# Second attention: the banks of the early projections, and the place of the matmuls that sum the probabilities

## The chip, the cores and the metric

The kernel runs on one core of a Trainium2 chip. Its time is the device time of one execution in microseconds (us); before the change the median of three runs is 2448.55 us (2448.41 to 2448.85). Five engines work side by side: PE (TensorE, matmuls; its weight loads stand in the profile as PEld), DVE (VectorE), ACT (ScalarE), POOL (GpSimd) and SP (SyncE, which issues the DMAs). Each engine runs its own list of instructions in order, and semaphores join them. Matmuls write to PSUM, which is eight banks of 128 x 512 fp32; DVE and ACT read the results from there.

## What is computed

The reference is four layers, each an attention and a feed-forward part, on x of 4 x 256 x 256 with a context of 4 x 1601 x 256. The change touches only the attention of the layer numbered 2, "the second attention":

```python
q = rms_norm((x @ wq).reshape(B, L, 16, 128), q_norm_w)
k, v = x @ wk, x @ wv                      # 4 heads of 128
k_ctx, v_ctx = ctx @ wk_ctx, ctx @ wv_ctx  # 4 heads of 128; k and k_ctx through rms_norm
q, k = q * cos + rotate_half(q) * sin, k * cos + rotate_half(k) * sin
scores = einsum(q, concat([k_ctx, k])) / sqrt(128) + causal
out = einsum(softmax(scores), concat([v_ctx, v]))
return out.reshape(B, L, 2048) @ wo
```

Each key head serves four query heads. There are 1601 + 256 keys, which make 15 chunks of up to 128.

## The kernel before

The second attention runs in 16 **turns**, one for each batch and key head (`TURNS = B * KH`), with a turn ahead of them that only prepares. Turn g does the attention of head g and beside it prepares head n = g + 1. A turn has 29 **steps** (`NS`), one for each pair of a tile of 128 queries (k = 0, 1) and a chunk of keys it sees: 14 steps for k = 0 (c = 0 to 13) and 15 for k = 1 (c = 14 to 28). The order of the work is written out by hand, by step, for each engine.

At step c of turn g, PE issues in this order:
- `project` (L1654 to L1671): at steps 2 to 16, the projection of one chunk of keys and values of the **next** head, two matmuls of 256 columns in fp32, which run as four passes (L1670). At steps 23 and 25 a projection of queries (L1651) instead.
- `search` (L1757 to L1766): one or two pieces of the maximum search of the next head, from step 11 on; the first before or after the scores, the second behind the values (L1764, L1765).
- `scores` of step c + 3 (L1699 to L1701), into banks 0 to 2 in turn.
- `values` of step c (L1704 to L1718): three matmuls of 512 columns, V high with P high (L1715), V low with P high (L1716), V high with P low (L1718), which add into bank 3 for k = 0 and bank 4 for k = 1.
- `sums` (L1720 to L1728): the probabilities of a query tile, added up on POOL in `l2_acc` (L1322), are summed over the keys by four matmuls of one column, fp32, so eight weight loads and eight passes (L1727). Those of k = 0 stand at step 21 of the same turn, those of k = 1 at step 1 of the next (`SUM_AT = [21, 1]`), behind the values of that step; at step 21 behind the second search piece too.
- `output` (L1747), `maxima` (L1754, at step 6 for k = 1 and step 24 for k = 0) and the transposes of the preparation (L1777, L1790).

A projection or search piece takes its PSUM bank from a list, `BANKS` (L1213), which goes by the item's place in the order `SHARED`. Before the change the first 23 items (the projections of steps 2 to 16 and the eight search pieces among them) go to banks 5 and 6 in turn, the rest to 3, 5, 6. `bank_free` (L1631) makes PE wait, ahead of the item's first weight load, until the last earlier item of the same bank has been read. For a projection that is the DVE subtraction that makes V low (L1533), which follows two ACT copies (L1422, L1423); for a search piece the DVE maximum (L1540). The first item on a bank in a turn waits for the last one of the turn before; the first on bank 3 waits on `l2_o` for the ACT copy of the finished k = 0 output.

That copy is `products` (L1401 to L1404): ACT reads bank 3 or 4 into `l2_oT` and adds one to `l2_o`. That of k = 0 runs at step 15 of its turn, that of k = 1, which reads bank 4, at step 1 of the **next** turn (`PV_AT`), where it stands behind `exp` of step 3 (L1364, L1365) and the seed of a score bank (L1376) in ACT's order.

Of the kernel before, what the change touches and what calls it, by code (L numbers as in the profile page):

```python
# [17 lines left out]
P = 128  # L18
B, S, D = 4, 256, 256
DC = D // P  # L20
TB = S // P
# [63 lines left out]
def program(nc, t, out):  # L85

    with ExitStack() as stack:

        def sem(name):
            return stack.enter_context(nc.semaphore(name))  # L90
# [4 lines left out]
        def sb(name, shape, dt=F32, scope=stack):  # L95
            return scope.enter_context(nc.sbuf_tensor(name, shape, dt))
# [3 lines left out]
        def bank(n, width=BANK, at=0):  # L100
            return psum[:, n * BANK + at:n * BANK + at + width]
# [12 lines left out]
        ones = sb("ones", [P, P])  # L114
# [25 lines left out]
        x_upd = sem("x_upd")  # L140
# [3 lines left out]
        xT_cp = sem("xT_cp")  # L144
# [10 lines left out]
        X_AT = [sum(UPDATES[:k]) for k in range(len(UPDATES) + 1)]  # L155
# [948 lines left out]
        KG = -(-KC // 4)  # L1104
# [3 lines left out]
        TURNS = B * KH  # L1108
# [14 lines left out]
        l2_acc, l2_oT = parts[:TB], parts[TB:]  # L1123
# [38 lines left out]
        NS = len(STEPS)  # L1162
        TILE_END = [max(c for c in range(NS) if STEPS[c][0] == k) for k in range(TB)]
# [22 lines left out]
        SUM_AT = [21, 1]  # L1186
        Y_AT = [(26, 28), (3, 5)]
        LAST_SUM, LAST_Y = 5, [(7, 6), (7, (NS - 3) % 3)]

        def max_pieces(c):  # L1190

            return [(k, h, q) for k, q, first, n in SEARCH_AT.get(c, []) for h in range(first, first + n)]
# [13 lines left out]
        def shared_at(c):  # L1206

            return ([("project", c)] if TB <= c < NPROJ else []) + [("query", k) for k in range(TB) if QUERY_AT[k] == c] \
                + [("search", SEARCH.index(piece)) for piece in max_pieces(c)]

        SHARED = [item for c in range(NS) for item in shared_at(c)]
        PAIR = sum(len(shared_at(c)) for c in range(NPROJ))
        BANKS = [5 + at % 2 for at in range(PAIR)] + [(3, 5, 6)[(at - PAIR) % 3] for at in range(PAIR, len(SHARED))]  # L1213
        EARLY_PROJECTS = 3
        FIRST_SHARED = [("project", k) for k in range(TB)] + SHARED
        LAST_ON_FIVE = TB + sum(len(shared_at(c)) for c in range(LATE_FROM))
# [3 lines left out]
        def is_first(n):  # L1220

            return isinstance(n, int) and n == 0

        def sequence(n):

            return (FIRST_SHARED, FIRST_BANKS) if is_first(n) else (SHARED, BANKS)

# [12 lines left out]
        def last_in(n, b, before=None):  # L1240

            items, of = sequence(n)
            return max((at for at in range(before or len(items)) if of[at] == b and (following(n) is not None or items[at][0] != "query")),
                       default=-1)
# [386 lines left out]
        def bank_free(pe, kind, i, n):  # L1631
            items, of = sequence(n)
            own = items.index((kind, i))
            at = last_in(n, of[own], own) if own else -1
            if at >= 0:
                wait_freed(pe, items[at], n)
            elif is_first(n):
                if own >= LAST_ON_FIVE:
                    pe.wait_ge(h_cp, HALF_CP[1])
            elif of[own] == 3:  # L1640
                pe.wait_ge(l2_o, (n - 1) * TB + 1)
            else:
                wait_freed(pe, sequence(n - 1)[0][last_in(n - 1, of[own])], n - 1)

# [28 lines left out]
        def l2x_tensor(pe):  # L1673
# [27 lines left out]
                pe.matmul(dst, l2_kTlo[slot][:, keys], l2_qThi[slot][:, k, :], start=False, stop=True, skip_group_check=True)\  # L1701
                    .then_inc(l2_s, 1)

            def values(g, slot, c):  # L1704
                k, j = STEPS[c]
                r = key_cols(j)[1]
                pe.wait_ge(l2_e, g * (3 * NS) + (3 * c + 1))
                if j == 0:
                    need(pe, l2_o, g * TB + (k - 1))
                if j == 0 and last_in(g, 3 + k) >= 0:  # L1710
                    wait_freed(pe, sequence(g)[0][last_in(g, 3 + k)], g)
                if k == 0:
                    pe.wait_ge(l2_vl, g * KC + (CHUNK_AT[j] + 1))
                vhi, vlo, phi = l2_vhi[slot][0:r, j, :], l2_vlo[slot][0:r, j, :], l2_phi[c % 3][0:r, :]
                pe.matmul(bank(3 + k), vhi, phi, start=(j == 0), stop=False)  # L1715
                pe.matmul(bank(3 + k), vlo, phi, start=False, stop=False)  # L1716
                pe.wait_ge(l2_lo, g * NS + (c + 1))
                pe.matmul(bank(3 + k), vhi, l2_plo[c % 3][0:r, :], start=False, stop=(j == MC + k)).then_inc(l2_pv, 1)  # L1718

            def sums(g, k, at=7):  # L1720
                pe.wait_ge(l2_accd, g * NS + (TILE_END[k] + 1))
                if at == LAST_SUM:
                    pe.wait_ge(xT_cp, TOP_CP + DONE // TB)
                elif k == 1:
                    pe.wait_ge(x_upd, g * (2 * TB) + (X_AT[4] + 2))
                for h in range(REP):
                    mm = pe.matmul(bank(at, 1, h), l2_acc[k][:, h * P:(h + 1) * P], ones[:, 0:1], start=True, stop=True)  # L1727
                mm.then_inc(l2_sum, 1)  # L1728

            def output(g, k, half):  # L1730
# [62 lines left out]
            def turn(g, slot, n):  # L1793
                for c in range(NS):
                    pieces = max_pieces(c) if n is not None else []
                    if n is not None and c >= (EARLY_PROJECTS if g is None else TB):
                        project(pe, c, n)
                    if c in QUERY_AT and following(n) is not None:
                        k = QUERY_AT.index(c)
                        if k == 0:  # L1800
                            weights_here(pe, n + 1)
                        bank_free(pe, "query", k, n)
                        project_query(pe, k, bank(shared_bank(n, "query", k)))
                    keys_turned = c - 1 in KT_AT.values()
                    if pieces and not keys_turned:
                        search(1 - slot, n, *pieces[0])
                    at, step = ahead(c, 3, g, n)
                    if at is not None:
                        scores(at, slot if c + 3 < NS else 1 - slot, step)
                    if pieces and keys_turned:  # L1810
                        search(1 - slot, n, *pieces[0])
                    if g is not None:
                        values(g, slot, c)
                    for piece in pieces[1:]:
                        search(1 - slot, n, *piece)
                    if g is not None:
                        later = not isinstance(g, int) or g >= 1
                        if c == SUM_AT[1] and later:
                            sums(g - 1, 1)
                        for half in range(2):  # L1820
                            if c == Y_AT[1][half] and later:
                                output(g - 1, 1, half)
                        if c == M1_AT:
                            if later:
                                pe.wait_ge(x_upd, g * (2 * TB) + X_AT[4])
                            maxima(g, 1)
                        if c == SUM_AT[0]:
                            if n is not None:
                                pe.wait_ge(l2_kTl, (n + 1) * KG)
                            sums(g, 0)  # L1830
                    if c == M_AT and n is not None:
                        if g is not None:
                            pe.wait_ge(l2_inv, g * TB + 1)
                        else:
                            pe.wait_ge(l2_kTl, (n + 1) * KG)
                        maxima(n, 0)
                    if g is not None:
                        for half in range(2):
                            if c == Y_AT[0][half]:
                                if n is not None and half == 0:  # L1840
                                    pe.wait_ge(l2_md, n * NSHIFT + 1)
                                output(g, 0, half)
                    if n is not None:
                        prepare(c, 1 - slot, n)
                    if last_turn(g) and c in XT_AT:
                        top_turn(pe, XT_AT[c])
                    if g is None and c == SECOND_HALF_AT[3]:
                        pe.wait_ge(h_xn, len(BLOCKS) + 2)
                        for d in range(DC):
                            attention_turn(pe, 1, d, 3 + d)  # L1850

            l2_turns_written_out(turn)
            sums(TURNS - 1, 1, LAST_SUM)
            for half in range(2):
                output(TURNS - 1, 1, half)

# [41 lines left out]
        DONE = NT - TB  # L1898
# [3 lines left out]
        TOP_K, TOP_PS, TOP_CP = norm_count["k"], norm_count["ps"], norm_count["cp"]  # L1902
# [1356 lines left out]
```

## Time and profile before

| | |
|---|---|
| median of three runs | 2448.55 us |
| the profiled execution, its own time | 2449.79 us |
| its span in the profile | 2448.0 us |
| the second attention | about 520 to 1745 us of the span |
| one full turn | 75.0 us |

Times in the rows are microseconds from the start of the span. A row of the timeline gives the start, the duration, the engine, the line and the operation with its output, inputs and shape; xN stands for N such instructions in a row, whose duration is then that from the start of the first to the end of the last. In square brackets is the idle time ahead of it and what ended it. The end of a matmul is modelled and overlaps the next one, so that for PE it is the distance from start to start that counts. A weight load is drawn from the moment it begins.

### The profile page before, as it was taken

The numbers are of one execution on the slowest core, as the hardware profiler recorded it, in microseconds if no ns is written. First come the engines' busy times: TensorE is split into PE (matmuls) and PEld (weight loads), VectorE is DVE, ScalarE is ACT, GpSimd is POOL, SyncE is SP. The second block draws the span as 40 slices with busy tenths as digits, with TensorE's granted clock in tenths as the row PEclk, the third lists the DMA queues.
The fourth block names the chain that finished last, engine by engine and source line by source line (L and its number), as shares of the span: only waits on it lengthen the run. The fifth ranks groups of instructions, "written<-read, shape, count | busy, mean of one in ns | idle before, by whom it ended". The sixth has DMA issues, their size and how long they took to land.

```text
span 2448.0 us, 50586 instructions
## 1 busy us (share of the span) xinstructions
PE 2331.0 (95%) x19062; PEld 1628.8 (67%) x19123; DVE 1740.0 (71%) x3346; ACT 1739.6 (71%) x3784; POOL 1327.3 (54%) x942
## 2 busy tenths in 40 slices
PE   7989999989999999999999999999799799999997
PEld 4677777767777777777777777777655444444444
DVE  5455767668988888888889888889411666666546
ACT  2235444458888888888888888888411688888897
POOL 1035555435666766666766667666500487878500
PEclk9989999999999999999999999999899999999999
DMA  5222322230001000010000100003200200000100
GB/s 189 70 85 84 91 86 81 78 138 13 6 18 49 18 18 1 18 49 18 18 3 17 49 18 18 18 1 138 89 28 11 72 25 16 23 17 22 55 3 18
DMA packets 42321, 108.36 MB, mean 44 GB/s; under 512 B 5060, under 2 KB 25928, under 8 KB 36936
## 3 DMA queue, kind: packets, MB, share of 16 engines
q1 hardware_dynamic: 40312, 102.28, 12.4%
q8 instruction: 156, 2.56, 0.5%
q0 software_dynamic: 768, 2.10, 0.3%
q10 hardware_dynamic: 1008, 0.79, 0.1%
q14 instruction: 77, 0.63, 0.1%
HBM read 99.78 MB, written 4.98 MB: 43 GB/s over the span
## 4 chain that ended last, share of the span: by engine, by line
PE 70%; DVE 11%; ACT 11%; issue 4%; POOL 2%; DMA 0%; another core or an unknown queue 0%; SPq 0%; ACTq 0%; DVEq 0%; POOLq 0%
PE psum L1670 6%; PE psum L2820 4%; PE psum L1765 4%; PE psum L1699 3%; PE psum L1715 3%; PE psum L1716 3%; PE psum L1718 3%; PE psum L2787 3%; PE psum L1700 3%; PE psum L1701 3%; PE psum L2184 3%; ACT l_p L2623 3%; PE psum L2753 3%; PE psum L513 2%; PE psum L515 2%
## 5 line engine op out<-in xcount | busy, mean ns | idle before, releaser
L1322 POOL TENSOR_TENSOR xn<-xn,l_p 128x512 f32<-128x512 f32 (+1 forms) x400 | 562.1, 1405 | 320.1 <-DVE l_plo L1490 308.0
L1490 DVE TENSOR_TENSOR l_plo<-l_p,l_phi 128x512 fp32r<-128x512 f32 (+1 forms) x464 | 440.4, 949 | 10.6 <-ACT l_p L1365 9.5
L2623 ACT ACTIVATE l_p<-psum 128x1024 f32<-128x1024 f32 x416 | 397.6, 1038 | 55.9 <-PE psum L2787 51.2
L1364 ACT ACTIVATE l_phi<-psum 128x512 fp32r<-128x512 f32 (+1 forms) x464 | 276.1, 595 | 100.8 <-PE psum L1701 60.1
L1540 DVE TENSOR_REDUCE l_mx<-psum 128x1 f32<-128x512 f32 (+2 forms) x512 | 303.7, 615 | 53.4 <-PE psum L1765 53.0
L1376 ACT ACTIVATE psum<-l_m 128x512 f32<-128x512 f32 x461 | 283.0, 616 | 7.9
L2598 POOL TENSOR_TENSOR l_rs<-l_ms,half_power 128x32 f32<-128x32 f32 x45 | 244.3, 5430 | 68.8 <-DVE l_ms L2648 58.7
L1365 ACT ACTIVATE l_p<-psum 128x512 f32<-128x512 f32 (+1 forms) x464 | 276.5, 596 | 0.0
L2820 PE MATMUL psum<-l_p,l_vs 64*32 64x256 f32 x6656 | 252.0, 378 | 6.9 <-POOL l_vs L2594 3.0
L1699 PE MATMUL psum<-l_qThi,l_kThi 128*128 128x512 f32 (+1 forms) x464 | 224.0, 483 | 0.9 <-ACT psum L1376 0.9
L1765 PE MATMUL psum<-l_kThi,l_qThi 128*128 128x512 f32 (+2 forms) x512 | 215.8, 450 | 6.8 <-ACT l_kThi L1457 2.3
L1670 PE MATMUL psum<-l_w,l_ctx 128*128 128x256 f32 (+1 forms) x832 | 217.6, 384 | 0.8 <-DVE l_vlo L1533 0.8
L597 POOL TENSOR_TENSOR w_lo_gu<-w_stage,w_hi_gu 128x512 fp32r<-128x512 f32 x76 | 99.7, 1312 | 163.3 <-ACT w_hi_gu L639 163.3
L1718 PE MATMUL psum<-l_plo,l_vhi 128*128 128x512 f32 (+1 forms) x464 | 184.5, 398 | 2.9 <-DVE l_plo L1490 2.9
L1715 PE MATMUL psum<-l_phi,l_vhi 128*128 128x512 f32 (+1 forms) x464 | 183.5, 395 | 0.0
L1716 PE MATMUL psum<-l_phi,l_vlo 128*128 128x512 f32 (+1 forms) x464 | 182.9, 394 | 0.0
L1700 PE MATMUL psum<-l_qTlo,l_kThi 128*128 128x512 f32 (+1 forms) x464 | 182.8, 394 | 0.0
L1701 PE MATMUL psum<-l_qThi,l_kTlo 128*128 128x512 f32 (+1 forms) x464 | 182.8, 394 | 0.0
L2787 PE MATMUL psum<-l_qT,l_kT 64*32 64x512 f16 x3328 | 171.9, 385 | 9.9 <-DVE l_qT L2447 1.5
L1670 PEld LDWEIGHTS psum<-l_w,l_ctx 128*128 128x128 f32 (+1 forms) x832 | 146.2, 187 | 25.6 <-DVE l_vlo L1533 5.9
L2820 PEld LDWEIGHTS psum<-l_p,l_vs 64*32 64x32 f32 x6656 | 118.6, 106 | 49.2 <-issue 8.5
L1765 PEld LDWEIGHTS psum<-l_kThi,l_qThi 128*128 128x128 f32 x512 | 97.7, 191 | 54.1 <-issue 23.2
(410 smaller groups left out, 5068.2 us busy)
## 6 DMA issues: line engine op xcount, KB each, us to landing
w_stage<-in_L_w_dram SPq DMA_DIRECT2D x76, 384.0 KB, 3.1
l_w<-in_L_w_qkv_dram SPq DMA_DIRECT2D x16, 1024.0 KB, 5.0
l_ct<-in_ctx_tiles_dram SPq DMA_DIRECT2D x52, 128.0 KB, 2.3
c_T<-in_ctx_T_dram SPq DMA_DIRECT2D x4, 1601.0 KB, 7.9
l_ctx<-in_ctx_T_dram SPq DMA_DIRECT2D x4, 1601.0 KB, 6.9
c_N<-in_ctx_dram SPq DMA_DIRECT2D x4, 1536.0 KB
s_wg<-in_L_gate_dram SPq DMA_DIRECT2D x4, 1024.0 KB, 10.8
s_wu<-in_L_up_dram SPq DMA_DIRECT2D x4, 1024.0 KB, 12.8
```

The source lines that it names most:

```text
L1322: g_.tensor_tensor(l2_acc[k][0:r, :], first[0:r, :], p_of(c)[0:r, :], ALU.add)\
L1364: act.activation(l2_phi[c % 3][0:r, :], src, ACT.Exp).then_inc(l2_e, 1)
L1365: act.activation(p_of(c)[0:r, :], src, ACT.Exp)\
L1376: return act.activation(bank(c % 3), l2_shift[:, STEPS[c][0], :].bitcast(F32), ACT.Copy)
L1490: v.tensor_tensor(l2_plo[c % 3][0:r, :], p_of(c)[0:r, :], l2_phi[c % 3][0:r, :].bitcast(F32), ALU.subtract)\
L1540: v.tensor_reduce(l2_mx4[:, u, q:q + 1], bank(shared_bank(n, "search", i), z - a), AX.X, ALU.max)\
L1670: mm = pe.matmul(into, lhs, l2_w[:, d, cols], start=(d == 0), stop=(d == DC - 1))
L1699: pe.matmul(dst, l2_kThi[slot][:, keys], l2_qThi[slot][:, k, :], start=False, stop=False, skip_group_check=True)
L1718: pe.matmul(bank(3 + k), vhi, l2_plo[c % 3][0:r, :], start=False, stop=(j == MC + k)).then_inc(l2_pv, 1)
L1765: pe.matmul(bank(at, z - a), l2_qThi[slot][:, k, h * P:(h + 1) * P], l2_kThi[slot][:, a:z], start=not masked, stop=True).then_inc(l2_near, 1)
L2623: act.activation(l3_p[ring(odd, c)][:, :], psum[:, (c % 2) * 2 * BANK:(c % 2 + 1) * 2 * BANK], ACT.Exp, scale=float(D3) ** -0.5).then_inc( ...
L2820: mm = pe.matmul(bank(at[a], S, cols)[h * 32:(h + 1) * 32, :], l3_vs[n % 2][rows, j, h, :], l3_p[s % 4][rows, h * S:(h + 1) * S], start=(j ...
```

## The change

Three things change.
- **Banks.** The first 11 items (the projections of steps 2 to 11 and the search piece of step 11) go to banks 4, 5 and 6 in turn. Items 11 to 22 go to 5 and 6 in turn, beginning with 5. The rest is as before. For the first projection on bank 4, that of step 2, `bank_free` waits on `l2_o` for the copy of the last turn's k = 1 output.
- **Sums.** `sums` is gone from its place; `values` takes its four matmuls in. Head 0 stands behind the first value matmul, head 1 behind the second, heads 2 and 3 behind the third. At step 21 they come ahead of the second search piece.
- **Waits.** The waits that stood ahead of `sums` (on `l2_accd`, on `x_upd` for k = 1, on `l2_kTl` for k = 0) now stand before or behind the first value matmul.

```diff
-        BANKS = [5 + at % 2 for at in range(PAIR)] + [(3, 5, 6)[(at - PAIR) % 3] for at in range(PAIR, len(SHARED))]
+        THREE_TILL = sum(len(shared_at(c)) for c in range(TILE_END[0] - 1))
+        BANKS = [4 + at % 3 for at in range(THREE_TILL)] + [5 + (at - THREE_TILL) % 2 for at in range(THREE_TILL, PAIR)] + [(3, 5, 6)[(at - PAIR) % 3] for at in range(PAIR, len(SHARED))]
...
             elif of[own] == 3:
                 pe.wait_ge(l2_o, (n - 1) * TB + 1)
+            elif of[own] == 4 and n > 1:
+                pe.wait_ge(l2_o, (n - 1) * TB)
             else:
...
-            def values(g, slot, c):
+            def sums_ready(g, k):
+                pe.wait_ge(l2_accd, g * NS + (TILE_END[k] + 1))
+                if k == 1:
+                    pe.wait_ge(x_upd, g * (2 * TB) + (X_AT[4] + 2))
+
+            def sum_head(k, h):
+                return pe.matmul(bank(7, 1, h), l2_acc[k][:, h * P:(h + 1) * P], ones[:, 0:1], start=True, stop=True)
+
+            def values(g, slot, c, summed, of):
...
                 pe.matmul(bank(3 + k), vhi, phi, start=(j == 0), stop=False)
+                if summed is not None:
+                    sums_ready(of, summed)
+                    sum_head(summed, 0)
                 pe.matmul(bank(3 + k), vlo, phi, start=False, stop=False)
+                if summed is not None:
+                    sum_head(summed, 1)
                 pe.wait_ge(l2_lo, g * NS + (c + 1))
                 pe.matmul(bank(3 + k), vhi, l2_plo[c % 3][0:r, :], start=False, stop=(j == MC + k)).then_inc(l2_pv, 1)
+                if summed is not None:
+                    sum_head(summed, 2)
+                    sum_head(summed, 3).then_inc(l2_sum, 1)
...
-                    if g is not None:
-                        values(g, slot, c)
+                    if g is not None and c == SUM_AT[0]:
+                        if n is not None:
+                            pe.wait_ge(l2_kTl, (n + 1) * KG)
+                        values(g, slot, c, 0, g)
+                    elif g is not None:
+                        values(g, slot, c, 1 if c == SUM_AT[1] and g >= 1 else None, g - 1)
```

## Rows read from the trace of the kernel before

**Rows 1.** The page: busy times, and the clock of PE in 40 slices.
```profile
PE 2331.0 (95%) x19062; PEld 1628.8 (67%) x19123; DVE 1740.0 (71%) x3346; ACT 1739.6 (71%) x3784; POOL 1327.3 (54%) x942
PEclk9989999999999999999999999999899999999999
```
**Rows 2.** Window of one turn: length; busy PE, PEld, DVE, ACT, POOL; granted clock, DMA share, GB/s.
```profile
795.37:870.37 75.00, 74.51 (x341) 57.55 (x342) 64.53 (x112) 64.52 (x177) 49.81 (x37) 1.00 0.04 15
```
**Rows 3.** Waits of PE's weight loads, 645 to 1695: us, times, longest.
```profile
PEld psum L1764 <- issue: 28.6, 84, 0.7
PEld psum L1754 <- DVE x L1506: 5.7, 14, 0.4
PEld psum L1670 <- DVE l_vlo L1533: 3.4, 14, 0.2
```
**Rows 4.** Timeline of PE over steps 1 and 2 of a turn.
```profile
793.65 0.39 PE L1716 MATMUL psum<-l_phi,l_vlo 128*128 128x512 f32 x1
793.88 0.40 PE L1718 MATMUL psum<-l_plo,l_vhi 128*128 128x512 f32 x1
794.11 0.95 PE L1727 MATMUL psum<-ones,xn 128*128 128x1 f32 x8
```
**Rows 5.** Timeline of the weight loads of the same steps.
```profile
793.65 0.19 PEld L1718 LDWEIGHTS psum<-l_plo,l_vhi 128*128 128x128 f32 x1
793.88 1.09 PEld L1727 LDWEIGHTS psum<-ones,xn 128*128 128x128 f32 x8
794.89 0.63 PEld L1670 LDWEIGHTS psum<-l_w,l_ctx 128*65 128x65 f32 x4
```
**Rows 6.** Timeline of ACT up to the k = 1 copy of that turn.
```profile
788.61 0.60 ACT L1364 ACTIVATE l_phi<-psum 128x512 fp32r<-128x512 f32 x1 [2.35 <-PE psum L1701]
...
794.85 0.60 ACT L1376 ACTIVATE psum<-l_m 128x512 f32<-128x512 f32 x1
795.39 0.58 ACT L1404 ACTIVATE xn<-psum 128x512 f32<-128x512 f32 x1
```
**Rows 7.** Timeline of the same place ten turns later.
```profile
1545.25 0.63 PEld L1670 LDWEIGHTS psum<-l_w,l_ctx 128*65 128x65 f32 x4
...
1545.75 0.58 ACT L1404 ACTIVATE xn<-psum 128x512 f32<-128x512 f32 x1
```
**Rows 8.** Timeline of DVE and PEld at steps 11 and 12.
```profile
820.94 0.29 DVE L1533 TENSOR_TENSOR l_vlo<-psum,l_vhi 128x128 fp32r<-128x128 f32 x1
821.08 0.40 PE L1718 MATMUL psum<-l_plo,l_vhi 128*128 128x512 f32 x1
821.15 0.35 DVE L1540 TENSOR_REDUCE l_mx<-psum 128x1 f32<-128x194 f32 x1
821.29 0.73 PEld L1670 LDWEIGHTS psum<-l_w,l_ctx 128*128 128x128 f32 x4 [0.25 <-DVE l_vlo L1533]
```
**Rows 9.** Timeline around the maxima of step 6.
```profile
807.06 0.99 DVE L1506 SCALAR_TENSOR_TENSOR x<-psum,l_rec,x 128x256 f32<-128x256 f32 x2
807.75 0.39 PE L1718 MATMUL psum<-l_plo,l_vhi 128*128 128x512 f32 x1
808.10 0.19 PEld L1754 LDWEIGHTS psum<-l_diag,l_minus 128*128 128x128 f32 x1 [0.40 <-DVE x L1506]
808.21 0.85 PEld L1670 LDWEIGHTS psum<-l_w,l_ctx 128*128 128x128 f32 x4
```
**Rows 10.** Timeline at step 21: values, second search piece, sums.
```profile
845.98 0.40 PE L1718 MATMUL psum<-l_plo,l_vhi 128*128 128x512 f32 x1
...
846.23 0.19 PEld L1765 LDWEIGHTS psum<-l_kThi,l_qThi 128*128 128x128 f32 x1 [0.29 <-issue]
846.35 1.07 PEld L1727 LDWEIGHTS psum<-ones,xn 128*128 128x128 f32 x8
```
**Rows 11.** Timeline of PE at step 13, the longest wait of a turn.
```profile
826.58 0.40 PE L1718 MATMUL psum<-l_plo,l_vhi 128*128 128x512 f32 x1
827.25 0.24 PE L1764 MATMUL psum<-causal,identb 128*128 128x194 bf16 x1 [0.28 <-DVE l_vlo L1533]
```

## What the change should do to the time

> **What bounds the kernel now.** I read the page first: PE is busy for 95% of the span, DVE and ACT for 71% each, and the clock granted to PE is 90% of full or more in all but two slices [rows 1]. Busy time of PE is modelled, so I went on to a window of one turn. There PE is busy for 74.5 of 75.0 us, DVE and ACT for 64.5, at a granted clock of 1.00 (the higher level, 2.4 GHz), with the DMA engines at 4% [rows 2]. PE has the least room, and what counts is how its matmuls follow each other. In the timeline the value matmuls start 0.23 us apart, 793.65, 793.88, 794.11 [rows 4], and each weight load begins as the matmul before it begins [rows 4, 5]: the load of L1718 at 793.65, where the matmul of L1716 starts, the first of L1727 at 793.88, where that of L1718 starts. So a load is one matmul ahead and is hidden under 512 columns. Where a load waits for a semaphore, PE loses the delay and also the load, some 0.11 us.
>
> Then I asked which loads wait. In the list of waits of the weight loads [rows 3], the projections (L1670) have one entry only: 14 times in 14 turns, at most 0.2 us. That is the projection of step 12. The other projections start their loads with the matmul before them, though banks 5 and 6 alone serve them. The costly waits are elsewhere: search pieces (L1764; the longest, at step 13, has the matmul at 827.25 where the one before it, 826.58, allows 826.81 [rows 11]), and the maxima of step 6 behind the DVE additions (L1754) [rows 3]. A third bank has no wait of a projection to take away but that at step 12, and there the change gives two banks.
>
> **The change, part by part.**
>
> *Bank 4 for the projection of step 2.* This is the dear one. Item 0 moves from bank 5 to bank 4, and bank 4 holds the k = 1 output of the last turn until ACT has copied it (L1404). ACT does that at its own step 1: in the turn shown from 795.39 to 795.97 [rows 6]. PE loads the first weights of the projection at 794.89 [rows 5]. Ten turns later the two stand the same way, load at 1545.25, copy from 1545.75 for 0.58 [rows 7]. The copy can't come sooner: ACT runs its list in order, starts at 788.61 when scores arrive from PE (after 2.35 us without work), and then works through exps and seeds without a pause to the copy [rows 6], so it keeps its distance from PE. From a DVE read that ends to the load that it releases takes 821.29 - 821.23 = 0.06 us [rows 8]. The load therefore moves from 794.89 to about 796.03, and PE stands still for **1.14 us** in each turn with n > 1 that still prepares a head: g = 1 to 14, 14 turns. Behind the waiting load are, in PE's order, the whole step: projection, scores of step 5, values of step 2. ACT has exp 4 to do meanwhile. Bounds: 0.9 us, if the semaphore tells the load 0.2 us before the record of the copy ends; 1.4 us, if the matmul's own load has to be added and the copy is a little later.
>
> *What of it comes back.* At step 6 the maxima wait for two DVE additions (L1506) that end at 808.05; the load comes at 808.10, and the next one, at 808.21, marks the matmul's start, against 807.75 + 0.23 = 807.98 [rows 9]. That is 0.23 us lost per turn. DVE is behind PE here, working on older steps, so that it doesn't move with PE. With PE 1.14 us later the wait is over before PE gets there: **-0.23 us**, 14 times. The waits further on are chains that begin on PE (transposes or a projection, ACT copy, DVE, PE again), the 0.44 us at step 13 among them [rows 11]; they move with PE and stay. Bounds: nothing comes back, or up to all 1.14.
>
> *The other early projections.* Banks 4, 5, 6 for steps 3 to 11: no wait is there to be removed, so 0.
>
> *The seam between the two lists.* Item 10, the search piece of step 11, gets bank 5 (4 + 10 mod 3), and item 11, the projection of step 12, gets 5 too (the second list begins with 5). Before, that projection waited for V low of step 11, which ends at 820.94 + 0.29 = 821.23. Now it waits for the maximum of the search piece, which DVE does right behind, to 821.15 + 0.35 = 821.50 [rows 8]. PE was just held up here already (load at 821.29 where 821.08 was possible), so the whole difference counts: **+0.27 us** in 15 turns (g = 0 to 14). From item 13 on both lists go round the same two banks with the numbers swapped: each item waits for the same one as before, so 0; items 12, 24 and 25 change their partner and didn't wait.
>
> *Sums between the values.* Eight passes of one column take from 793.88 (first load) to 794.89 (next load): the first load lies under L1718, the other seven and the one that follows start about 0.11 us apart [rows 4, 5]. The price is the loads. A group of n such passes between two large matmuls has n + 1 loads, its own and the next matmul's, and one of them is hidden. One group of 8 exposes 8 loads; groups of 2, 2 and 4 expose 2 + 2 + 4 = 8. So **0**, 31 times (16 at step 21, 15 at step 1). The third value matmul ends 0.45 us later and releases a P buffer later, but the exp that needs it is two ACT steps of about 1.8 us away. Bounds for a group: -0.9 us (all eight loads hidden) and +0.2 (two more loads exposed).
> The Trainium skill, page "TensorE: Matmul & The Clock Gate", section "Step-by-step: what each phase is for", says that the PE's 64-deep window pulls weight loads ahead of matmuls in flight. Taken literally, with many loads pulled ahead, that would make the sums nearly free; the trace disagrees, since no load runs more than one matmul ahead.
>
> *The second search piece of step 21* now comes behind the sums. Before, its load waited until 846.23, and the matmul could start at 846.34 where 845.98 + 0.23 = 846.21 was possible [rows 10]. It waits for a maximum that DVE has done by then, so 0.9 us later it waits for nothing: **-0.13 us**, 15 turns.
>
> *Waits moved forward.* At step 1 the sum of k = 1 needs POOL's last addition and the DVE additions of step 28, at step 21 the last V and K parts. They were free of waiting, with no idle time in front of the eight passes [rows 4, 5], and move by at most 0.5 us. I take 0; bounds 0 and +0.3 each.
>
> **The sum.** 14 x (1.14 - 0.23) + 15 x (0.27 - 0.13) = 12.7 + 2.1 = 14.8 us. Against the profiled execution's own 2449.79 us that is 2464.6; it stands 1.24 us above the median of 2448.55, and from the median I get **2463.4 us**, 0.6% slower.
>
> **The rivals.**
> - *PE makes up for the stall.* The three waits listed come to 37.7 us of waiting loads in 14 turns, 2.7 us a turn, nearly all ahead of search pieces [rows 3]. If they come from DVE and ACT being behind rather than from chains that begin on PE, a PE that is 1.14 us late meets none of them and the stall costs nothing. Then 2448.55 + 15 x 0.14 = 2450.7, within 0.2%. For it: DVE is behind PE around step 6. Against: DVE and ACT have 10 us of idle time in the turn [rows 2], so they catch up before step 13.
> - *The sums get free.* The one mechanism for a gain: weight loads of one-column passes hidden under the value matmuls around them. All eight: 31 x 0.9 = 28 us, so 2463.4 - 28 = 2435. It decides from 0.48 us for a group, over four of eight loads, where the 14.8 us are paid. For it: the large matmul lasts 0.23 us, twice a load. Against: a load begins only when the matmul before it begins [rows 4, 5], so there is room for one.
> - *The stall spreads.* Step 6 gives nothing back and the late PE also costs ACT a little at exp 5: 14 x 0.23 + 14 x 0.1 = 4.6 us more, 2468.
> - That the change doesn't start a projection sooner is part of the forecast: none waited.
>
> The Trainium skill, "Perfetto Trace Analysis", section "Optimization Strategy", says that the same gap coming back on the engine that should be saturated can mean too few buffers in PSUM. By it a third bank should help. The gap is there, but not at the projections: all that their waits could give is 3.4 us over 14 turns [rows 3], and that sits at step 12, where the change leaves two banks.
>
> **How the numbers follow.** Forecast 0.72 (own range 2459 to 2467); PE makes up for it 0.13; sums free 0.07; stall spreads 0.08. The range that leaves out no more than 2 in 10 reaches from the forecast down to the recovery and up to the spreading: 2450 to 2469. A measurement can tell 0.2% from no change, which is 4.9 us: faster is below 2443.7, slower above 2453.4. Slower 0.80, same 0.13, faster 0.07.
>
> **What would show it.** In the trace of after: at step 2 the load of L1670 idle for over 1 us behind ACT L1404, in 14 turns; the turn at 76.0 to 76.1 us instead of 75.0; L1754 no longer waiting for L1506; at step 12 L1670 waiting for L1540 instead of L1533, 0.3 us later against its predecessor; from the first value matmul of step 1 (793.65 - 0.23 = 793.42) to the end of the last sum as long as before (to 794.89, 1.47 us). I am wrong if that stretch shrinks, if the copy L1404 comes earlier against PE, or if the waits of L1764 shrink by as much as step 2 loses.

## The result

| | before | after |
|---|---|---|
| median | 2448.7 us (2448.4 to 2451.0, 4 runs) | 2467.8 us (2463.5 to 2469.1, 4 runs) |
| profiled execution, its own time | 2449.79 us | 2467.95 us |
| its span | 2448.0 us | 2466.2 us |

The ratio after to before is 1.0076 (95% interval 1.0063 to 1.0089). The change makes the kernel slower by 0.76%, some 18.6 us (the medians differ by 19.1). The forecast was 14.8 us and 2463.4 us, with 2450 to 2469 as the range.

The page of after says little about the cause. It answers to [rows 1] with busy times that have hardly moved; PE did the same work (19123 weight loads in both) and is as busy as before, over a longer span:

```profile
PE 2332.6 (95%) x19123; PEld 1630.4 (66%) x19123; DVE 1746.8 (71%) x3346; ACT 1745.2 (71%) x3784; POOL 1325.1 (54%) x942
PEclk9989999999999999999999999999899999999999
```

The first view to open is the windows. I cut both spans at the first and at the last weight load for a value matmul of the second attention. Columns as in [rows 2]; first before, then after:

```profile
0.00:567.36 567.36, 522.78 (x2253) 393.15 (x2280) 358.20 (x693) 244.87 (x511) 218.41 (x220) 0.97 0.30 97
567.36:1740.86 1173.50, 1159.67 (x5262) 893.45 (x5293) 1006.99 (x1713) 1011.65 (x2711) 786.08 (x567) 1.00 0.07 25
1740.86:2448.00 707.14, 648.60 (x11550) 342.23 (x11551) 374.83 (x942) 483.09 (x564) 322.85 (x156) 0.98 0.10 33
```
```profile
0.00:567.28 567.28, 522.91 (x2279) 392.70 (x2279) 358.18 (x693) 245.09 (x511) 218.82 (x220) 0.97 0.30 97
567.28:1760.33 1193.05, 1161.68 (x5294) 896.53 (x5293) 1014.04 (x1713) 1017.19 (x2711) 783.20 (x567) 1.00 0.07 25
1760.33:2466.20 705.87, 647.97 (x11553) 341.12 (x11551) 374.61 (x942) 482.96 (x564) 323.09 (x156) 0.98 0.10 33
```

The middle stretch, the attention itself, is 1193.05 - 1173.50 = 19.5 us longer at the same granted clock (1.00), with 2 us more of PE busy time (32 more of its matmul records are in this trace, for the same number of loads); the rest is PE standing still. The stretches at its sides do what they did. One turn of after, answering to [rows 2], is 1.4 us longer:

```profile
797.62:874.04 76.42, 74.67 (x343) 57.77 (x342) 64.99 (x112) 64.89 (x177) 49.60 (x37) 1.00 0.05 15
```

The list of waits of the weight loads, over the same turns as [rows 3], names the places (us, times, longest):

```profile
PEld psum L1673 <- ACT xn L1405: 14.8, 14, 1.1
PEld psum L1673 <- DVE l_mx L1541: 13.8, 14, 1.0
```

Line numbers move by 1 to 16 in after: the projection is L1673 (was L1670), ACT's copy L1405 (L1404), the search maximum L1541 (L1540), the first value matmul L1726 (L1715). The two entries are new: the projection of step 2 waits for ACT's copy of bank 4, and that of step 12 for the maximum of the search piece with which it now shares bank 5. The entries for L1754 behind DVE and for L1670 behind V low in [rows 3] are gone.

**By step.** Since the profile has the load of the first value matmul of every step, a turn can be laid out step by step: the distance from that load to the one of the next step. The table gives the median over the turns g = 2 to 13. All steps that are not in it agree within 0.03 us, and the turns differ among themselves by 0.05 us at most at these steps.

| step | what lies in it | before | after | difference | forecast |
|---|---|---|---|---|---|
| 1 | sums, then the projection of step 2 | 3.10 | 4.22 | +1.12 | +1.14 |
| 6 | maxima | 2.73 | 2.49 | -0.24 | -0.23 |
| 11 | projection of step 12 | 2.44 | 3.18 | +0.74 | +0.27 |
| 13 | second search piece | 3.08 | 2.84 | -0.25 | 0 |
| 21 | sums, second search piece | 2.83 | 2.83 | 0 | -0.13 |
| turn | | 75.05 | 76.44 | +1.39 | +1.05 |

14 turns x 1.39 = 19.5 us, which is what the windows show. In turn g = 0, where no copy is to be waited for, the only differences above 0.04 us are +0.27 at step 11 and -0.26 at step 13: nothing in sum.

**Step 1 to 2 in the trace.** After's weight loads at the place of [rows 4 and 5], and ACT's copy at that of [rows 6]:

```profile
796.15 0.42 PEld L1713 LDWEIGHTS psum<-ones,xn 128*128 128x128 f32 x2
796.49 0.19 PEld L1730 LDWEIGHTS psum<-l_phi,l_vlo 128*128 128x128 f32 x1
796.60 0.42 PEld L1713 LDWEIGHTS psum<-ones,xn 128*128 128x128 f32 x2
796.94 0.19 PEld L1734 LDWEIGHTS psum<-l_plo,l_vhi 128*128 128x128 f32 x1
797.05 0.65 PEld L1713 LDWEIGHTS psum<-ones,xn 128*128 128x128 f32 x4
798.75 0.62 PEld L1673 LDWEIGHTS psum<-l_w,l_ctx 128*65 128x65 f32 x4 [1.05 <-ACT xn L1405]
```
```profile
798.13 0.58 ACT L1405 ACTIVATE xn<-psum 128x512 f32<-128x512 f32 x1
```

Read the starts. The two loads of head 0 and that of V low take 796.15 to 796.60, 0.45 us, where a value matmul alone takes 0.23: the one-column passes add two loads of 0.11 each. The eight passes end where four loads from 797.05 (the matmul before them streams for 0.23 us, three more loads of 0.11) would let the next one start, at 797.62; from the start of the first value matmul, 796.15, that is 1.47 us, as it was. Then nothing until 798.75, 1.13 us: the copy runs from 798.13 to 798.71, and the load follows its end by 0.05 us.

### The profile page after: what moved, and what is told of

It reads as the page before. It is cut to its first block, busy times and chain, and to the rows that moved or that the text cites. A ratio compares the mean times of both kernels' runs of the same rounds, so it can differ in the third digit from the quotient of the medians.

```text
span 2466.2 us, 50647 instructions
## 1 busy us (share of the span) xinstructions
PE 2332.6 (95%) x19123; PEld 1630.4 (66%) x19123; DVE 1746.8 (71%) x3346; ACT 1745.2 (71%) x3784; POOL 1325.1 (54%) x942
## 4 chain that ended last, share of the span: by engine, by line
PE 70%; ACT 11%; DVE 11%; issue 5%; POOL 1%; DMA 1%; ACTq 0%; SPq 0%; DVEq 0%; POOLq 0%
PE psum L1673 7%; PE psum L1781 4%; PE psum L2834 4%; PE psum L1726 3%; PE psum L1734 3%; PE psum L1730 3%; PE psum L1702 3%; PE psum L1703 3%; PE psum L1704 3%; PE psum L2801 3%; PE psum L2198 3%; ACT l_p L2637 3%; PE psum L2767 3%; PE psum L513 2%; PE psum L515 2%
## 5 line engine op out<-in xcount | busy, mean ns | idle before, releaser
L1491 DVE TENSOR_TENSOR l_plo<-l_p,l_phi 128x512 fp32r<-128x512 f32 (+1 forms) x464 | 452.0, 974 | 10.7 <-ACT l_p L1366 9.5
L1541 DVE TENSOR_REDUCE l_mx<-psum 128x1 f32<-128x512 f32 (+2 forms) x512 | 303.7, 614 | 53.4 <-PE psum L1781 53.0
L1673 PE MATMUL psum<-l_w,l_ctx 128*128 128x256 f32 (+1 forms) x832 | 218.3, 385 | 22.1 <-ACT xn L1405 13.6
L1781 PE MATMUL psum<-l_kThi,l_qThi 128*128 128x512 f32 (+2 forms) x512 | 214.3, 451 | 6.8 <-ACT l_kThi L1458 2.3
L1726 PE MATMUL psum<-l_phi,l_vhi 128*128 128x512 f32 (+1 forms) x464 | 183.9, 396 | 0.0
L1673 PEld LDWEIGHTS psum<-l_w,l_ctx 128*128 128x128 f32 (+1 forms) x832 | 146.0, 186 | 51.8 <-ACT xn L1405 14.8
L2801 PEld LDWEIGHTS psum<-l_qT,l_kT 64*32 64x32 f16 x3328 | 48.3, 90 | 126.6 <-ACT l_p L2637 87.5
```

Source lines behind the costliest of these rows:

```text
L1491: v.tensor_tensor(l2_plo[c % 3][0:r, :], p_of(c)[0:r, :], l2_phi[c % 3][0:r, :].bitcast(F32), ALU.subtract)\
L1541: v.tensor_reduce(l2_mx4[:, u, q:q + 1], bank(shared_bank(n, "search", i), z - a), AX.X, ALU.max)\
L1673: mm = pe.matmul(into, lhs, l2_w[:, d, cols], start=(d == 0), stop=(d == DC - 1))
L1781: pe.matmul(bank(at, z - a), l2_qThi[slot][:, k, h * P:(h + 1) * P], l2_kThi[slot][:, a:z], start=not masked, stop=True).then_inc(l2_near, 1)
L2801: mm = pe.matmul(bank(s % 2 * 2 + a)[r:r + 32, :], l3_kT[b % 2][rows, n, j * P + r:j * P + r + 32], queries, start=True, stop=True)
```

## The experiments

Each was run beside the kernel before on the same chip. Times of single executions spread by several us, and nearly all of that is in the stretch ahead of the second attention: in the profiles of all these kernels it ends between 562.1 and 573.1 us of the span, while the middle stretch of those whose turn stays at 75.05 us is within 0.3 us of before's. The verdicts therefore rest on the steps, as in the table above, and the medians stand beside them.

**Sums alone.** The kernel before with after's `values`; banks and `bank_free` as before.

```diff
-        BANKS = [4 + at % 3 for at in range(THREE_TILL)] + ...
+        BANKS = [5 + at % 2 for at in range(PAIR)] + ...
-            elif of[own] == 4 and n > 1:
-                pe.wait_ge(l2_o, (n - 1) * TB)
```

> The kernel before with the sums between the value matmuls and nothing else. Theory (the loss is PE's wait for ACT's copy of bank 4, and the sums cost what they did): the turn stays at 75.05 us, within 0.1 us, and the time within 1 us of before, 2447.7 to 2449.7. Rival (the sums between the values cost, through two more exposed loads or through their waits, which now stand among the value matmuls): 31 groups at 0.2 us, +6 us. Rival (their loads get hidden): up to -28 us.

Measured: 2447.7 us, ratio 1.000 (0.9989 to 1.0011); turn 75.04 us, no step differs by 0.03 us. The middle stretch in its windows, 0.2 us longer than before:

```profile
562.07:1735.80 1173.73, 1160.01 (x5262) 894.46 (x5294) 1007.21 (x1713) 1012.37 (x2711) 785.79 (x567) 1.00 0.07 25
```

Moving the sums between the values costs nothing and brings nothing. Both rivals are out.

**Banks alone.** The kernel before with after's `BANKS` and its wait on `l2_o`.

```diff
-        BANKS = [5 + at % 2 for at in range(PAIR)] + ...
+        BANKS = [4 + at % 3 for at in range(THREE_TILL)] + [5 + (at - THREE_TILL) % 2 ...] + ...
+            elif of[own] == 4 and n > 1:
+                pe.wait_ge(l2_o, (n - 1) * TB)
```

> The kernel before with the new banks and nothing else; the sums stay behind the values. Theory: all of the loss is here. Step 1 to step 2 +1.12 us, step 6 -0.24, step 11 +0.7, step 13 -0.25 in 14 turns, 2448.7 + 19 = 2468. Rival (the sums' place carries the part of step 11 that was not forecast, +0.47 of its +0.74): 14 x 0.47 = 6.6 us less, 2461.

Measured: 2469.6 us, ratio 1.0081 (1.0064 to 1.0098); turn 76.42; steps 1, 6, 11, 13: +1.12, -0.23, +0.73, -0.24. The whole loss is in the banks.

**Another bank first.** After, with the first list turned round.

```diff
-        BANKS = [4 + at % 3 for at in range(THREE_TILL)] + ...
+        BANKS = [(5, 6, 4)[at % 3] for at in range(THREE_TILL)] + ...
```

> The kernel after with the first list turned round: banks 5, 6, 4 in place of 4, 5, 6. Bank 4 is then first asked for at step 4, when the copy has been over for some 4 us, and items 10 and 11 no longer share a bank. Theory: no wait for the copy, no seam; the turn is back at 75.05 us or up to 0.1 less, 2447 to 2449. Rival (a third bank costs as such, by letting PE run ahead into DVE and POOL's work): the turn stays above 75.3, the time above 2453.

Measured: 2450.1 us, ratio 1.0001 (0.9991 to 1.0011); turn 75.06, no step differs. Three banks cost nothing when bank 4 is asked for two steps later; they bring nothing either, since up to step 11 there was no wait to remove.

**The copy a step earlier.** After's banks, and ACT copies the k = 1 output at step 0.

```diff
-        PV_AT = [TILE_END[0] + 2, 1]
+        PV_AT = [TILE_END[0] + 2, 0]
```

> The kernel after with ACT's copy of the k = 1 output one step earlier, at step 0 instead of step 1; the banks are those of after. Theory: the copy ends some 1.7 us sooner, before PE asks for bank 4, so the 1.12 us go, and with them what step 6 gave back; with PE no longer late, step 11 costs 0.27 and step 13 gives back 0.26, as in the first turn of after, where there is no copy to wait for. Turn 75.1, time 2449. Rival (the copy is not what PE waits for, or ACT falls behind elsewhere by the same 0.6 us): the turn stays over 76.

Measured: 2448.1 us, ratio 1.0001 (0.9991 to 1.0011); turn 75.03; step 1 and step 6 as before, step 11 +0.27, step 13 -0.25. The copy is now over while PE still loads for the sums:

```profile
790.10 0.58 ACT L1405 ACTIVATE xn<-psum 128x512 f32<-128x512 f32 x1
790.21 0.42 PEld L1713 LDWEIGHTS psum<-ones,xn 128*128 128x128 f32 x2
790.58 0.59 ACT L1365 ACTIVATE l_phi<-psum 128x512 fp32r<-128x512 f32 x1
```

(The second ACT row is the exp of the next step, right behind.) So the wait of PE is for this copy and for nothing else, and with it gone the seam costs exactly the 0.27 us of the forecast. The other 0.47 us of step 11 need a late PE.

**The seam mended.** After, with the second list begun at bank 6; the wait for the copy stays.

```diff
-  [5 + (at - THREE_TILL) % 2 for at in range(THREE_TILL, PAIR)]
+  [6 - (at - THREE_TILL) % 2 for at in range(THREE_TILL, PAIR)]
```

> The kernel after with the second list begun at bank 6, so that items 10 and 11 no longer share bank 5; the wait for the copy stays. Theory: step 1 +1.12 us and step 6 -0.24 as in after; step 11 no longer waits for the search piece's maximum, so its +0.74 is gone and the time lost there before, 0.08, too; step 13 stays at -0.1 to -0.25. Turn 75.7 to 75.9, time 2459. Rival (the step 11 loss comes from PE being late, not from the shared bank): the turn stays near 76.4.

Measured: turn 75.73; step 1 +1.12, step 6 -0.24, step 11 -0.08, step 13 -0.15. The middle stretch is 9.7 us longer than before's (19.5 in after). The single time of 2465.8 us is above the expected 2459: this execution's stretch ahead of the attention was 5.8 us longer than before's. Half of the loss hangs on the shared bank: the projection of step 12 now asks for bank 6, whose last item lies two steps further back, so that it waits for nothing (the 0.08 us that it lost before are gone too), and a late DVE can't hurt it.

**Why step 11 cost 0.74 and not 0.27.** DVE's timeline at steps 11 and 12 of after, to be held against [rows 8], and POOL's:

```profile
823.80 1.34 DVE L1491 TENSOR_TENSOR l_plo<-l_p,l_phi 65x512 fp32r<-65x512 f32 x1
825.06 0.28 DVE L1534 TENSOR_TENSOR l_vlo<-psum,l_vhi 128x128 fp32r<-128x128 f32 x1
825.26 0.34 DVE L1541 TENSOR_REDUCE l_mx<-psum 128x1 f32<-128x194 f32 x1
825.66 0.73 PEld L1673 LDWEIGHTS psum<-l_w,l_ctx 128*128 128x128 f32 x4 [0.98 <-DVE l_mx L1541]
```
```profile
823.55 1.04 POOL L1346 TENSOR_TENSOR l_kn<-l_kraw,l_krs 128x512 f32<-128x512 f32 x1
```

The subtraction L1491, ahead of V low in DVE's order, lasts 1.34 us. In the kernel before the same one, and POOL's scaling of the keys beside it:

```profile
820.16 0.68 DVE L1490 TENSOR_TENSOR l_plo<-l_p,l_phi 65x512 fp32r<-65x512 f32 x1
820.25 1.49 POOL L1345 TENSOR_TENSOR l_kn<-l_kraw,l_krs 128x512 f32<-128x512 f32 x1
```

Whichever of the two starts first keeps its time (DVE 0.68, POOL 1.04), and the other is drawn out. Before, DVE was 0.09 us ahead; in after it is 0.24 to 0.29 us behind, in each of the 14 turns. It comes 3.64 us later than before in the span (820.16, 823.80), POOL's operation only 3.30 us (820.25, 823.55): DVE's follows ACT's copy of keys that PE has turned, and PE is late, while POOL's follows an earlier DVE operation, which moved less. Of the 0.66 us that the subtraction gains in length 0.47 reach PE, since before V low was held until 820.92 by ACT's copy and not by the subtraction. To test it, POOL's operation was shortened; this kernel leaves three chunks of keys unscaled and doesn't compute the reference.

```diff
+                            nb = 1 if place == 1 else nb
                             g_.tensor_tensor(l2_kn[place % 2][:, 0:nb, :], l2_kraw[place % 2][:, 0:nb, :],
```

> The kernel after, with POOL's scaling of the second group of keys (L1346, the one at step 9 of the list, seen at 823.55) cut from four chunks to one; three chunks of keys stay unscaled, so the result is not the reference's. Theory (the part of step 11 that was not forecast, 0.47 us, is a DVE subtraction that lasts 1.34 instead of 0.68 us because this POOL operation is under way when it starts): with POOL done after about 0.3 us the DVE operation is back at 0.7 and step 11 is at 2.71, +0.27 against before. Rival (DVE is late for another reason, ACT's copy or a PE wait): step 11 stays at 3.18.

Measured: 2456.1 us in a single execution; turn 75.96; step 11 +0.27, the other steps as in after; the middle stretch 13.0 us longer than before's, which is 19.5 less 14 x 0.47. The rows:

```profile
817.65 0.40 POOL L1347 TENSOR_TENSOR l_kn<-l_kraw,l_krs 128x128 f32<-128x128 f32 x1
817.90 0.69 DVE L1492 TENSOR_TENSOR l_plo<-l_p,l_phi 65x512 fp32r<-65x512 f32 x1
```

POOL still starts 0.25 us ahead and DVE is back at 0.69. What is left of POOL's operation (0.15 us when DVE starts) is too short to draw it out. The meeting of the two operations is the cause of the 0.47 us.

**What a one-column pass costs.** Each sum matmul issued twice, once in the kernel of "Sums alone" (between the values) and once in the kernel before (behind them). These are single executions too.

```diff
             def sum_head(k, h):
+                pe.matmul(bank(7, 1, h), l2_acc[k][:, h * P:(h + 1) * P], ones[:, 0:1], start=True, stop=True)
                 return pe.matmul(bank(7, 1, h), l2_acc[k][:, h * P:(h + 1) * P], ones[:, 0:1], start=True, stop=True)
```

> Sums between the values, banks as before, and each of the four sum matmuls issued twice: 8 more passes in each of 31 groups and in the last. Theory (each one-column pass costs one weight load of 0.11 us on PE, wherever it stands): steps 1 and 21 longer by 8 x 0.112 = 0.90 us each, the turn 76.85, time 2448.7 + 28 = 2476.5. Rival (loads are hidden under the value matmuls around them): under 0.5 us a step.

```diff
                 for h in range(REP):
-                    mm = pe.matmul(bank(at, 1, h), l2_acc[k][:, h * P:(h + 1) * P], ones[:, 0:1], start=True, stop=True)
+                    for twice in range(1 if at == LAST_SUM else 2):
+                        mm = pe.matmul(bank(at, 1, h), l2_acc[k][:, h * P:(h + 1) * P], ones[:, 0:1], start=True, stop=True)
```

> The kernel before with each sum matmul issued twice, the sums behind the values as before. Theory: the same 0.90 us at steps 1 and 21 as between the values, turn 76.85, time 2476.5. Rival (the place matters): a step costs more here than between the values.

Measured: between the values, step 1 +0.88 and step 21 +0.88, time 2474.3 us, turn 76.81; behind them +0.89 and +0.90, 2476.4 us, turn 76.80. The loads, first between, then behind:

```profile
796.89 0.42 PEld L1710 LDWEIGHTS psum<-ones,xn 128*128 128x128 f32 x2
...
799.25 0.41 PEld L1670 LDWEIGHTS psum<-l_w,l_ctx 128*65 128x65 f32 x3
```
```profile
799.26 0.19 PEld L1716 LDWEIGHTS psum<-l_phi,l_vlo 128*128 128x128 f32 x1
799.49 0.19 PEld L1718 LDWEIGHTS psum<-l_plo,l_vhi 128*128 128x128 f32 x1
799.72 1.99 PEld L1728 LDWEIGHTS psum<-ones,xn 128*128 128x128 f32 x16
801.63 0.41 PEld L1670 LDWEIGHTS psum<-l_w,l_ctx 128*65 128x65 f32 x3
```

From the start of the first value matmul to the next projection's load: 799.25 - 796.89 = 2.36 us and 801.63 - 799.26 = 2.37 us. A pass costs 0.11 us wherever it stands. Both kernels show something more: their banks are those of before, yet steps 6, 11 and 13 move by -0.23, +0.48 and -0.25, which are after's -0.24, its +0.74 less the 0.27 of the shared bank, and its -0.25. PE is late behind step 1 here too, for another reason, and the late PE alone brings the meeting of DVE and POOL.

**A version from what was learnt.** Bank 5 first, and the third bank kept up to the projection of step 14, so that it reaches the places where PE did wait.

```diff
-        THREE_TILL = sum(len(shared_at(c)) for c in range(TILE_END[0] - 1))
-        BANKS = [4 + at % 3 for at in range(THREE_TILL)] + ...
+        THREE_TILL = SHARED.index(("project", TILE_END[0] + 1)) + 1
+        BANKS = [(5, 6, 4)[at % 3] for at in range(THREE_TILL)] + ...
```

> The kernel after with banks 5, 6, 4 in turn for the first 17 items (up to the projection of step 14), then 5 and 6 in turn. Bank 4 is asked for after the copy is over, and the third bank now reaches the places where PE waited in the kernel before: the projection of step 12 (0.08 us, it had waited for V low of step 11), the second search piece of step 13 (0.44 us, for V low of step 13) and the projection of step 14 (0.08, for the maximum before it). With three banks the search piece waits for the piece of step 12, done long before, and the projection of step 14 for V low of step 13, which stays the last: some 0.26 of the 0.44 can come back, since its end at 827.11 and not 827.37 opens the bank. Theory: turn 74.7, the second attention 15 x 0.34 = 5 us shorter than before, time 2443.6, ratio 0.998. Rival (DVE and POOL's work moves by as much and PE meets the same wait at the next item): turn 75.0, no difference.

Measured: 2445.1 us (11 runs) against 2448.8 (15 runs), ratio 0.9983 (0.9974 to 0.9992); turn 74.81; step 11 -0.08, step 13 -0.17, the attention 3.5 us shorter. It beats both kernels, by less than expected. Its rows at step 13:

```profile
825.82 0.19 PEld L1734 LDWEIGHTS psum<-l_plo,l_vhi 128*128 128x128 f32 x1
826.29 0.10 PEld L1780 LDWEIGHTS psum<-causal,identb 128*128 128x128 bf16 x1 [0.28 <-issue]
826.38 0.28 DVE L1534 TENSOR_TENSOR l_vlo<-psum,l_vhi 128x128 fp32r<-128x128 f32 x1
826.71 0.73 PEld L1673 LDWEIGHTS psum<-l_w,l_ctx 128*128 128x128 f32 x4 [0.21 <-DVE l_vlo L1534]
```

The search piece (L1780) now goes before V low of step 13 is done, but the projection of step 14 meets the same V low one item later, at 826.38 + 0.28 + 0.05 = 826.71: of the 0.44 us of [rows 11] 0.17 came back.

## Why the prediction was right, and where its sum was short

The direction, the place and the main term were right, and the time lies in the stated range. It lies 0.8 us above the 2459 to 2467 that the forecast kept for its own mechanism, and close to the 2468 of the rival that let the stall spread, which is in part luck: what was missing came from another place.

- **Bank 4 and ACT's copy: right**, in cause and size. Forecast 1.14 us in 14 turns, measured 1.12 in the same 14; undone by another bank first or by an earlier copy, each by itself.
- **Step 6 gives back 0.23: right.** Measured 0.24, and it stays away when PE is not late (the copy a step earlier).
- **The seam, 0.27: right as a price of the bank, wrong as the price in after.** It is 0.27 in turn 0 of after and in the kernel with the early copy, and 0.74 in the 14 turns with a late PE. The step that failed is "the whole difference counts": it took DVE's durations of [rows 8] as fixed. The end of V low moved by another 0.47 us because a DVE operation ahead of it met POOL. This is the largest miss, 14 x 0.47 = 6.6 us.
- **Step 13, "they move with PE and stay": wrong** by 0.25 us. In [rows 11] PE waits for V low, behind a subtraction that lasts 0.90 us before and 0.68 in after. POOL's additions and that subtraction, first before, then after:

```profile
821.71 4.58 POOL L1322 TENSOR_TENSOR xn<-xn,l_p 128x512 f32<-128x512 f32 x3
825.94 0.90 DVE L1490 TENSOR_TENSOR l_plo<-l_p,l_phi 128x512 fp32r<-128x512 f32 x1
```
```profile
824.55 4.84 POOL L1323 TENSOR_TENSOR xn<-xn,l_p 128x512 f32<-128x512 f32 x3
830.27 0.68 DVE L1491 TENSOR_TENSOR l_plo<-l_p,l_phi 128x512 fp32r<-128x512 f32 x1
```

Before, the subtraction starts 0.35 us ahead of POOL's end (826.29) and ends 0.55 us behind it, as nearly all such subtractions do (last section); in after POOL has been done since 829.39. The gain comes with the seam alone as well (turn 0, early copy) and with a late PE alone (the doubled sums). The rows fit, but no run took POOL away there: argued, not shown.
- **The sums, 0 at step 1: right**, to 0.03 us, and the mechanism behind it (one exposed load for each pass) was measured by itself.
- **Step 21, -0.13: wrong in size, measured 0.** The wait of the second search piece did go. But I had not counted what follows the group: before, the load behind the last of the eight is the bf16 one of L1764, and it begins only 0.03 us after it (at 847.26) instead of 0.11. In after a full load, that of the first search matmul (L1781, 851.16), stands behind the eight, 0.11 us after the last, and the bf16 one comes behind that matmul. That is 0.08 us of the 0.13; the small rest isn't taken apart.
- **The sum.** The terms as measured: 1.12 - 0.24 + 0.74 - 0.25 and 0.02 of small ones is 1.39 for a turn; the forecast had 1.05. The +0.47 that the forecast missed at step 11 is half taken back by the -0.25 that it missed at step 13; the absent -0.13 of step 21 makes up the rest.
- **The rivals.** PE did not make up for the stall; what came back is 0.24 of 1.12, and perhaps the 0.25 of step 13, which comes with a stall alone and with the seam alone. The 37.7 us of waiting loads on which this rival built were mostly no loss: of the 84 entries at L1764, 28.6 us in all, 70 show 0.27 to 0.28 us where PE goes on without a gap (one at 820.38, 0.24 us after the matmul ahead of it, started at 820.14). Only the 14 of step 13 cost time, the 0.44 us of [rows 11] each. The sums did not get free. Of the third, that the stall spreads, half came true, at another place than it named: not exp 5, but DVE and POOL at step 11.
- **The Trainium skill.** The Trainium skill, page "TensorE: Matmul & The Clock Gate", section "Step-by-step: what each phase is for", has weight loads pulled ahead of matmuls in flight. The trace agrees with it as far as the next tile's weights go, of which the section speaks as well: here it is one load and no more, and doubling the passes between large matmuls costs the full 0.11 us each. The Trainium skill, "Perfetto Trace Analysis", section "Optimization Strategy", says that a gap that comes back can mean too few buffers in PSUM. The trace agrees where such a gap was: the third bank brought 3.5 us at steps 12 to 14 and nothing at steps 2 to 11, where there was none.

## What to carry to other kernels

Before a bank or buffer is added to a rotation, look up who else holds it at the moment of its first use, and compare the end of that holder's read with the load that will ask for it; the same three banks gave +19.5, 0 or -3.5 us here, by their order and reach alone. Where two lists of a rotation meet, check the item on either side of the seam. Take a third bank to the items that wait, not to those that don't, and count each pass of a one-column matmul (two for a matmul in fp32 here) as one exposed weight load of 0.11 us wherever it stands.

## What the runs showed of the hardware

DVE's subtraction L1490 and POOL's additions and scalings (L1322, L1345), which all read and write SBUF, don't share the loss when they overlap: the one that starts first keeps its time, and the other ends a fixed time after it. Ahead of V low of step 11: DVE 0.68 us and POOL 1.49 with DVE 0.09 us ahead, DVE 1.34 and POOL 1.04 with POOL 0.25 us ahead; either way both are over 1.58 us after the first start, 0.14 less than the two in a row. The kept trace of before has 264 subtractions in the attention that start while such an operation of POOL has 0.15 us or more to go: 263 of them end 0.54 to 0.56 us after it, whatever was left of it, where the subtraction alone lasts 0.68. It doesn't hold for everything on POOL. Beside its power operation L1338 the subtraction keeps its time, 15 times out of 15:

```profile
794.67 2.10 POOL L1338 TENSOR_TENSOR l_qrs<-l_qms,half_power 128x8 f32<-128x8 f32 x1
795.18 0.69 DVE L1490 TENSOR_TENSOR l_plo<-l_p,l_phi 128x512 fp32r<-128x512 f32 x1
```

Here a shift of a third of a microsecond of one against the other made the subtraction 0.66 us longer, and 0.47 of it reached PE.

Also, the time of one execution varies by several us through the stretch ahead of the second attention (562 to 573 us), while a turn of 75 us repeats to 0.1 us (turns 1 to 13 of before: 74.98 to 75.10). A difference of 0.1% in such a stage is read from its steps, not from the total.
